# Attention loop of a decoder block: the maxima units and the value matmuls change places within a step

## What is computed

```python
q = q * cos + _rotate_half(q) * sin
k = k * cos + _rotate_half(k) * sin
attn = jnp.einsum('bhqd,bhkd->bhqk', q, k) * SCALE
diff = pos[None, :] - pos[:, None]
diff = jnp.where(diff > 0, 0.0, diff)
alibi = diff[None, :, :] * slopes[:, None, None] * MAX_BIAS
w = jax.nn.softmax(attn + alibi[None], axis=-1)
out = jnp.einsum('bhqk,bhkd->bhqd', w, v)
```

## Time and profile before

| | |
|---|---|
| median of the three timed runs | 1882.13 us (1870.05 to 1885.53) |
| time of the profiled execution | 1873.03 us, its span 1871.3 us |
| TensorE matmul busy | 1632.2 us, 87% |
| VectorE busy | 1304.5 us, 70% |
| ScalarE busy | 991.7 us, 53% |
| attention windows with maxima (15 of them) | about 155 to 871 us of the span |
| attention window without maxima | about 871 to 911 us |

### The profile page before, as it was taken

How to read it: one execution, slowest core, us unless ns; L and a number is a source line. 1 busy time by engine, 2 the same in 40 slices (tenths; PEclk the granted TensorE clock), 3 DMA queues, 4 the chain that set the end, 5 groups by cost and what they waited for, 6 DMA issues and landing times. The chain is left out here.

```text
span 1871.3 us, 36268 instructions
## 1 busy us (share of the span) xinstructions
PE 1632.2 (87%) x14816; PEld 1064.6 (57%) x14816; DVE 1304.5 (70%) x2288; ACT 991.7 (53%) x1692; POOL 403.7 (22%) x268
## 2 busy tenths in 40 slices
PE   7858999999999999999584799879985999999970
PEld 7734444444444444444274555546764888888870
DVE  6967888888888888886185547652334677777736
ACT  5324777777777777777534267844533333333310
POOL 6540000000000000000234101101452244444440
PEclk9967999999999999999798679978996999999995
DMA  7887444544444444430455968223213333344235
GB/s 260 216 214 198 65 68 62 69 64 67 66 62 66 67 65 65 63 45 9 141 194 182 116 94 132 76 76 108 84 39 109 75 90 92 93 94 94 38 34 180
DMA packets 131133, 183.85 MB, mean 98 GB/s; under 512 B 30886, under 2 KB 95284, under 8 KB 129912
## 3 DMA queue, kind: packets, MB, share of 16 engines
q1 hardware_dynamic: 117528, 159.47, 40.6%
q0 software_dynamic: 13440, 22.07, 5.7%
HBM read 114.86 MB, written 69.99 MB: 99 GB/s over the span
## 5 line engine op out<-in xcount | busy, mean ns | idle before, releaser
L694 DVE TENSOR_REDUCE att_row_max<-att_ring 128x2 f32<-128x1024 f32 x512 | 602.2, 1220 | 115.8 <-PE att_ring L760 57.1
L678 ACT ACTIVATE att_w_exp<-att_s_ps 128x512 f32<-128x512 f32 x999 | 536.2, 599 | 222.4 <-PE att_s_ps L807 150.3
L834 PE MATMUL att_a_ps<-att_w_exp,att_v_group 128*32 128x512 f32 x2048 | 273.6, 606 | 0.8 <-ACT att_acc_sb L667 0.6
L793 PE MATMUL att_s_ps<-att_q_stack,att_k_stack 62*128 62x512 f32 x640 | 182.0, 481 | 0.0
L793 PEld LDWEIGHTS att_s_ps<-att_q_stack,att_k_stack 62*128 62x128 f32 x640 | 84.4, 184 | 124.0 <-ACT att_w_exp L678 112.9
L2232 ACT ACTIVATE ex_hid<-ex_h_ps,ex_b 128x512 f32<-128x512 f32 x128 | 87.2, 686 | 118.0 <-DVE ex_h_lo L2287 65.9
L616 POOL COPY att_eyes<-keep_slope_eye 128x384 bf16<-128x384 bf16 x16 | 8.1, 511 | 642.7 <-PE att_s_ps L807 631.9
L2188 POOL DMA_INDIRECT x_scr<-ex_y,ex_home x64 | 107.0, 1671 | 182.3 <-DVE ex_y L2277 167.6
L2287 DVE TENSOR_TENSOR ex_h_lo<-ex_hid,ex_h_hi 128x512 fp32r<-128x512 f32 x128 | 138.6, 1083 | 4.4
L760 PE MATMUL att_ring<-att_k_stack,att_q_stack 60*128 60x512 f32 x640 | 131.5, 451 | 6.2 <-DVE att_att L721 3.2
L807 PE MATMUL att_s_ps<-att_eyes,keep_past_bf 64*128 64x64 bf16 x3738 | 130.6, 193 | 0.0
(11 more groups left out here) (303 smaller groups left out, 3549.9 us busy)
## 6 DMA issues: line engine op xcount, KB each, us to landing
first_w_raw<-ew SPq DMA_DIRECT2D x16, 1024.0 KB
att_k_stack<-qk_scr SPq DMA_DIRECT2D x120, 128.0 KB
cr_q_stack<-q_scr SPq DMA_DIRECT2D x48, 256.0 KB, 9.6
keep_k_stack<-qk_scr SPq DMA_DIRECT2D x72, 128.0 KB
rows_scr<-att_zeros POOLq DMA_DIRECT2D x8, 1040.0 KB, 22.2
first_rows<-rows_scr SPq DMA_DIRECT2D x16, 520.0 KB
att_q_stack<-qk_scr SPq DMA_DIRECT2D x60, 128.0 KB
qk_scr<-qkv_t_hi SPq DMA_DIRECT2D x7, 1024.0 KB, 4.3
```

What stands on the lines that cost most here:

```text
L678: nc.scalar.activation(w_exp[(STEPS * g.n + st) % SETS][h][:, :], score_bank(v), ACT.Exp).then_inc(exp_done, 1)
L694: nc.vector.tensor_reduce(out, ring[place.slot][:, :, :], AX.X, ALU.max).then_inc(ring_free, 1)
L793: ins = nc.tensor.matmul(score_bank(v), ks[g.buf][rows, c, j, kt * P:(kt + 1) * P], qs[g.buf][rows, j, c * CH:(c + 1) * CH], start=True, s ...
L834: ins = nc.tensor.matmul(a_ps[32 * h:32 * h + 32, :], vg[g.buf][:, kt, h * VW:h * VW + 32], w_exp[(STEPS * g.n + st) % SETS][h][:, :], sta ...
```

## The change

Within a step TensorE issues the two units of maxima between the two pairs of scores, and the values behind the second pair: pair 0, transposes, maxima, maxima, pair 2, values, where it was pair 0, values, transposes, pair 2, maxima, maxima. The transposes of accumulated values move from steps 2 and 10 to steps 3 and 11, with the matching entries of the ring and VectorE's normalisation. ScalarE's copy of the accumulated values moves from behind the second exponential of steps 1 and 9 to behind the first of steps 2 and 10. `max_unit` gives the half of keys so that the unit with diagonal bias is always the second of a step. No instruction is added or removed.

```diff
 def max_unit(u):
     half, rest = divmod(u, 16)
     pair, rest = divmod(rest, 8)
-    return half, pair, rest // 2, rest % 2
+    return half, pair, rest // 2, (rest + 1 + half) % 2
...
-        if st == 2 and not first:
+        if st == 3 and not first:
             order.append(("acc", 1))
...
-        if st == 10:
+        if st == 11:
             order.append(("acc", 0))
...
-                        if st == 1 and h == 1 and has_last:
+                        if st == 2 and h == 0 and has_last:
                             copy_acc(g.plus(-1), 1)
-                        if st == 9 and h == 1:
+                        if st == 10 and h == 0:
                             copy_acc(g, 0)
...
-                    if st == 2 and has_last:
+                    if st == 3 and has_last:
                         normalise(g.plus(-1), 1, PLACES[g.n, "acc", 1])
...
-                    if st == 10:
+                    if st == 11:
                         normalise(g, 0, PLACES[g.n, "acc", 0])
...
                     score_pair(g, st, 0)
+                    if st == 1:
+                        transpose_top(g, 1, PLACES[g.n, "top", 1])
+                    if st == 3 and has_last:
+                        transpose_acc(g.plus(-1), 1, PLACES[g.n, "acc", 1])
+                    if st == 9 and with_max:
+                        transpose_top(n, 0, PLACES[g.n, "top", 0])
+                    if st == 11:
+                        transpose_acc(g, 0, PLACES[g.n, "acc", 0])
+                    if with_max:
+                        for i in range(2):
+                            max_pair(n, 2 * st + i, PLACES[g.n, "max", 2 * st + i])
+                    score_pair(g, st, 2)
                     if st > 1:
                         values(g, st - 2)
                     elif has_last:
                         values(g.plus(-1), STEPS + st - 2)
-                    if st == 1:
-                        transpose_top(g, 1, PLACES[g.n, "top", 1])
-                    if st == 2 and has_last:
-                        transpose_acc(g.plus(-1), 1, PLACES[g.n, "acc", 1])
-                    if st == 9 and with_max:
-                        transpose_top(n, 0, PLACES[g.n, "top", 0])
-                    if st == 10:
-                        transpose_acc(g, 0, PLACES[g.n, "acc", 0])
-                    score_pair(g, st, 2)
-                    if with_max:
-                        for i in range(2):
-                            max_pair(n, 2 * st + i, PLACES[g.n, "max", 2 * st + i])
```

## The result

The changed kernel takes 1890.4 us in the median of 20 runs (1883.36 to 1906.4), the kernel before 1876.8 us (1869.5 to 1887.98, 20 runs beside them). The ratio is 1.0074, 95% interval 1.0056 to 1.0092: 0.7% slower, 13.6 us. The forecast was 1885 us, 7 us more than before. The time lies in the stated range and the change has the forecast sign, but the change is about twice the size that was forecast.

What follows compares the result with a forecast made beforehand. The prediction took a loop through one exponential, not TensorE, as the bound. Per window -0.06 + 0.39 + 0.14 = +0.47 us, together +7 us on a mean of 1877.7, gave 1885 us, range 1872 to 1902.

Steps and rivals of the forecast that it cites:

- The bound: Ordinary window steps are a closed loop through one exponential, 2.60 us plain and 2.99 biased; TensorE is not at its limit.
- The circle is the same: Ordinary steps: the new order is the old one with the pairs exchanged, still 2.60 and 2.99 us, so 0.
- Bias unit second: 0.: Units of maxima, diagonal bias in the second: any gain or loss stays inside the 0.25 us wait, so 0.
- step 1: Step where maxima are transposed: pair 2 at 1.54 instead of 1.38 us, +0.16, a gain of 0.06.
- Steps 3 and 11: +0.98 and +1.03: Steps where values are transposed: the second maxima unit waits for VectorE's normalisation, pair 2 0.98 and 1.03 us later.
- Step 9: 0.47 as before: The first maxima unit keeps its 0.47 us wait for the ring, and the transpose hides in it.
- ScalarE's copy: 0.06: Copy ahead of the exponentials of heads 1 to 3: values of step 10 wait for its end, +0.06 us.
- The turn out of the scores: Three transposes a window pay 0.09 us each on leaving the scores, 4 us of the forecast 7.
- The sum: +0.47 us per window, 6.6 us in fourteen windows, +0.1 in the first: together +7 us, chance 0.64.
- The transposes vanish in the wait: Rival: if VectorE frees the ring slot in time, transposes cost 0.7 us less a window, -10 us, 1868; chance 0.17.
- The loop becomes shorter: Rival: plain steps fall to 2.40 and biased ones to 2.74 us, -48 us, 1830; chance 0.06.
- ScalarE's copy: Rival: the copy amid four exponentials delays a waiting matmul by 0.5 us, twice in 15 windows, +14 us, 1899; chance 0.13.

Runs made afterwards that it cites:

- bias unit as before: The changed kernel with max_unit as in the kernel before, so units of half 0 have their bias first; a window of 48.37 us, 0.17 less than the changed kernel.

## Why the prediction was right, and where it was short

*The bound.* Right, and now shown rather than argued. An ordinary step is a loop through one exponential: 0.49 us at head 0 shows in full, at head 1 not at all, and 0.24 us of extra matmuls nearly vanish. TensorE's 98.8% in the earlier trace rows was no limit.

*The circle is the same.* Right: 2.60 and 2.99 to within 0.01, with the pairs exchanged.

*Bias unit second: 0.* Wrong, in both directions. Alone it gains 0.12 a window (step 9). With the moved transposes it costs 0.21 in step 3 and 0.15 in step 1 and gains 0.14 in step 9; a window loses 0.17 by it. My argument, that it lies inside the wait for the exponential, holds in ordinary steps only. In steps 1 and 3 the bound is the ring, and there the place of the bias blocks relative to the wait counts; in step 9 TensorE waits for VectorE, which starts its reductions sooner.

*Steps 3 and 11: +0.98 and +1.03.* The mechanism was right to the step: the transposes at 0.62 (forecast 0.61), the second unit 1.47 after them (forecast 1.47). The term that was too small is the last one, from the second unit to pair 2. I took 0.28 and 0.32 from second units in the earlier trace rows that followed the first without a wait and had 4 bias blocks; these are released by VectorE and have 8. Measured: 0.47 in both steps (509.65 to 510.12). The kernel before already had a nearer case behind the released unit of the earlier trace rows, with 4 blocks, and there it was 0.41, from 522.77 to the pair in these rows:

```profile
523.11 0.24 PE L768 MATMUL att_ring<-att_eyes,keep_past_bf 64*128 64x64 bf16 x4
523.18 0.49 PE L793 MATMUL att_s_ps<-att_q_stack,att_k_stack 62*128 62x512 f32 x2
```

Against the forecast that is +0.19 and +0.15, and the 0.13 of step 1 (0.41 instead of 0.28) is the same term. Of the 0.42 a window that the forecast lacks (3.12 - 2.70), the three make 0.47; step 9 gives back 0.14 and step 10 adds 0.10, which comes to 0.43.

*Step 9: 0.47 as before.* It was 0.33, the bias unit's 0.13 again. *ScalarE's copy: 0.06.* Step 10 costs 0.16 over its loop, of which the copy is 0.04. The other 0.12 is the second unit's wait for VectorE's reduction (528.60), for which the forecast had no term in this step.

*The turn out of the scores.* The transposes start 0.62 after a biased pair of 0.52 and 0.43 after a plain one of 0.33, so the 0.09 that the earlier trace rows showed for values holds for transposes as well. No run took it away by itself. The forecast let three transposes a window pay it; the two single ones cost 0.08 in step 1 and nothing in step 9 against their place behind the values.

*The sum.* With 0.86 instead of 0.47 a window, 14 windows make 12.0 instead of 6.6 us. The edges of the stage show 2 more in this pair of profiles, where I had put 0 with 1 to either side. Two executions of one kernel differ by 3.5 there (53.3 and 49.7), and the granted clock of the stretch 165 to 170 us differed too, 0.98 in the profile before and 0.60 in the one after. So these 2 us say nothing for or against the forecast.

*The rivals.* "The transposes vanish in the wait" fell by its own condition: the normalisation ended 1.41 after the transposes started, and the second unit had to wait for it. "The loop becomes shorter" did not happen: ordinary steps stayed at 2.60. "ScalarE's copy" costs 0.04.

## What to carry to other kernels

When a schedule is rotated, write it as a circle: what keeps its distance in the circle costs nothing, and only what changes its neighbours needs a price. A short instruction that another engine has to read before its buffer is free should stand as far ahead of the next user of that buffer as the order allows; here a pair of scores between the two was worth about half a microsecond in each of steps 3 and 11. And where an instruction waits, put the optional work ahead of it, not behind: in step 3 the same bias blocks were free on one side of the wait and cost 0.13 us on the other, and 0.08 more in the pair behind them.

## What the runs showed of the hardware

- A granted clock of 1.00 and a TensorE counted 97.8 to 98.8% busy went together with 0.2 to 0.25 us of unused time in each 2.6 us step. An extra pair of matmuls a step, 0.24 us where it showed, made plain steps 0.03 us longer on average, and the busy count went only from 97.82 to 98.27 of 100 us.
- From a unit of maxima (two f32 matmuls of 60 rows by 512 columns, side by side) to its first bias block it took 0.34 us when the unit came after a wait (509.65 to 509.99, kernel after) and also when it came directly behind the transposes (505.43 to 505.77, bias unit as before). Directly behind another unit it took 0.23 us (483.52 to 483.75 in the kernel before). So it was what ran ahead of the unit, and not the wait as such, that went with the longer time.
- Matmuls of scores turned to values or to transposes 0.09 us later than to maxima: 0.42 and 0.43 against 0.33 us behind a plain pair.
- The second of two exponentials queued back to back on ScalarE starts 0.48 to 0.50 us after the first though each is counted 0.59, so doubling one cost 0.49.
